# Macaron block on one core: attention's f32 products on quarters of the PE array, and no mask

## The reference, cut to what matters

```python
x = x + 0.5 * ffn(layernorm(x)); x = x + attn(layernorm(x)); x = x + 0.5 * ffn(layernorm(x))
# attn: 16 heads of 32 channels
q, k = relu(to_heads(q)), relu(to_heads(k))
v_pad = jnp.pad(v, ((0, 0), (0, 0), (0, 1), (0, 0)), constant_values=1.0)
vk = jnp.einsum('bhen,bhdn->bhed', v_pad, k)     # per head: 33 x 32, summed over the 512 tokens
out = jnp.einsum('bhed,bhdn->bhen', vk, q)       # per head: 33 values for each token
out = out[:, :, :-1] / (out[:, :, -1:] + 1e-15)
return out.reshape(B, C, N).transpose(0, 2, 1) @ w_proj.T + b_proj
```

## Time and profile before

| | us |
|---|---|
| median of 3 runs (906.39 to 907.36) | 907.1 |
| the profiled execution | 907.83 |
| its span, first to last instruction | 906.0 |
| PE busy | 882.5 (97%) |
| PEld busy | 422.6 (47%) |
| DVE busy | 477.5 (53%) |
| ACT busy | 373.8 (41%) |
| POOL busy | 72.9 (8%) |
| mean granted TensorE clock | 0.994 |

### The profile page before, as it was taken

How to read it: one execution, slowest core, us unless ns; L and a number is a source line. 1 busy time by engine, 2 the same in 40 slices (tenths; PEclk the granted TensorE clock), 3 DMA queues, 4 the chain that set the end, 5 groups by cost and what they waited for, 6 DMA issues and landing times.

```text
span 906.0 us, 11596 instructions
## 1 busy us (share of the span) xinstructions
PE 882.5 (97%) x4288; PEld 422.6 (47%) x4288; DVE 477.5 (53%) x978; ACT 373.8 (41%) x732; POOL 72.9 (8%) x106
## 2 busy tenths in 40 slices
PE   3899999999999999999999999999999999999998
PEld 2544443444444444455555546444444444444443
DVE  7988889844335444525373737454433434433332
ACT  6666666555434445212121212263333344443431
POOL 3110001200000000100000000010000000100000
PEclk9899999999999999999999999999999999999999
DMA  9886614998525678433231404133444433342235
GB/s 279 121 135 129 94 35 90 195 192 179 124 44 119 127 173 157 96 52 47 47 48 20 74 1 83 23 58 59 88 88 88 79 77 71 70 71 59 59 62 135
DMA packets 251383, 84.90 MB, mean 94 GB/s; under 512 B 237888, under 2 KB 240448, under 8 KB 251328
## 3 DMA queue, kind: packets, MB, share of 16 engines
q1 hardware_dynamic: 242704, 70.54, 41.2%
q0 software_dynamic: 3872, 4.72, 3.9%
q10 hardware_dynamic: 4752, 8.91, 3.0%
HBM read 25.43 MB, written 4.19 MB: 33 GB/s over the span
## 4 chain that ended last, share of the span: by engine, by line
PE 94%; DMA 3%; DVE 2%; ACT 1%; issue 0%; ACTq 0%; SPq 0%
PE gate_ps L1063 22%; PE up_ps L1063 22%; PE proj_ps L1077 22%; PE gate_ps L1166 7%; PE up_ps L1166 7%; PE proj_ps L1087 5%; PE proj_ps L1063 4%; PE proj_ps L1177 2%; DMA slots<-slots 1%; DMA xT<-xn 1%; PE sum_ps L1049 1%; PE gate_ps L1102 1%; PE up_ps L1102 1%; DVE slots L796 1%; DMA xs<-in_L_attn_x_dram 1%
## 5 line engine op out<-in xcount | busy, mean ns | idle before, releaser
L1077 PE MATMUL proj_ps<-down_w,slots 128*128 128x512 bf16 x960 | 211.4, 380 | 0.9 <-DMA slots<-slots 0.9
L1063 PE MATMUL gate_ps<-gu_w,xT 128*128 128x512 bf16 (+1 forms) x904 | 203.8, 369 | 2.9 <-DMA xT<-xn 2.9
L1063 PE MATMUL up_ps<-gu_w,xT 128*128 128x512 bf16 (+1 forms) x904 | 203.6, 369 | 0.0
L783 DVE SCALAR_TENSOR_TENSOR slots<-up_ps,silu 128x512 f32<-128x512 f32 x118 | 81.5, 690 | 170.7 <-PE up_ps L1063 153.1
L1077 PEld LDWEIGHTS proj_ps<-down_w,slots 128*128 128x128 f16 x960 | 93.8, 98 | 114.0 <-issue 1.4
L548 ACT ACTIVATE silu<-gate_ps 128x512 f32<-128x512 f32 x118 | 69.7, 590 | 171.4 <-PE gate_ps L1063 171.3
L1063 PEld LDWEIGHTS gate_ps<-gu_w,xT 128*128 128x128 f16 x904 | 86.6, 98 | 102.3 <-DMA xT<-xn 3.0
L1063 PEld LDWEIGHTS up_ps<-gu_w,xT 128*128 128x128 f16 x904 | 86.3, 98 | 99.2
L558 ACT ACTIVATE o_buf<-slots 128x512 f32<-128x512 f32 x128 | 80.4, 628 | 93.7 <-DVE slots L783 92.5
L805 DVE SCALAR_TENSOR_TENSOR xs<-proj_ps,xs 128x512 f32<-128x512 f32 x32 | 22.1, 691 | 134.1 <-PE proj_ps L1077 134.1
L796 DVE SCALAR_TENSOR_TENSOR slots<-slots,inv 128x512 f16<-128x512 f32 x124 | 90.9, 743 | 3.0 <-ACT slots L569 3.0
(11 more groups left out here) (103 smaller groups left out, 746.3 us busy)
## 6 DMA issues: line engine op xcount, KB each, us to landing
out_dram<-xs SPq DMA_DIRECT2D x16, 256.0 KB, 2.4
slots<-in_L_ffn_w_gate_up_dram ACTq DMA_DIRECT2D x6, 512.0 KB, 7.5
aw_raw<-in_L_attn_w_qkv_dram ACTq DMA_DIRECT2D x12, 256.0 KB, 3.0
aw_raw<-in_L_attn_w_qkv_dram SPq DMA_DIRECT2D x12, 256.0 KB, 3.1
xs<-in_L_attn_x_dram SPq DMA_DIRECT2D x2, 1024.0 KB, 6.3
slots<-slots SPq DMA_TRANSPOSE x76, 4.5
xs<-in_L_attn_x_dram ACTq DMA_DIRECT2D x1, 1024.0 KB, 11.8
aw_raw<-in_L_ffn_w_gate_up_dram POOLq DMA_DIRECT2D x4, 256.0 KB, 7.4
```

The lines of the kernel that those rows point to most:

```text
L783: nc.vector.scalar_tensor_tensor(out=h_rows(i, q), in0=bank(up_ps, j), scalar=GU_OUT, in1=silu_rows(j), op0=ALU.mult, op1=ALU.mult).then_i ...
L1063: mm = nc.tensor.matmul(bank(ps, j)[:, first:first + width], xT(m)[:, t, r, k, :], gu_w[:, k, c:c + width], start=(k + r == 0), stop=(k == ...
L1077: mm = nc.tensor.matmul(proj_ps[:, use % 2, :], h_turned(i)[:, r, j, :], down_w[:, j, :], start=(r + j == 0), stop=(r == 1 and j == HC - 1))
```

## The change

K with V uses the array as four column tiles: for each head of a group (`e` = 0 to 3) one matmul of 32 stationary columns and 33 moving ones writes partitions 32e to 32e+31 of `proj_ps`. Q with the result uses four row tiles: for each head the 32 rows of the queries against 33 columns, each row tile into a bank of its own. So 16 f32 matmuls become 64 for K with V in a block, and 4 become 16 for a token tile. The values are stored with a column of ones for every head. The mask, `mask4` and their seven instructions in the prologue (and `mask`'s first ones) go; DVE now only copies the K-V product (two copies for a block).

The order changes with it: K with V comes before the sixth pair of projections (`qkv(b, 5)`), and DVE's copies at the head of step `u` = 5. All of PSUM is now one tensor, and the outputs of a token tile take four banks (one pair's second gate and up bank, and the two of `sum_ps`), the same four for each tile: `attention_output(b, t)` waits until tile `t-1` has been emptied. `gate_done` is signalled at the last group's second head, `up_done` at the end. In block 0 the products of tiles 14 and 15 are split into halves, one half ahead of each token tile.

```diff
-KV_W = P + HPG
-V_W = P + 1
+V_W = HEAD + 1
+G_W = DC * V_W
@@ ScalarE, a token tile
-                    nc.scalar.activation(out_half(t), gate_ps[:, j % 2, 0:2 * KV_W], ACT.Copy).then_inc(gate_used, 1)
+                    nc.scalar.activation(out_half(t), banks[:, 2:4, 0:G_W], ACT.Copy).then_inc(gate_used, 1)
@@ VectorE, u == 5
+                    if u == 5:
+                        for half in range(2):
+                            dve.wait_ge(proj_done, KV_USE[b] + half + 1)
+                            nc.vector.tensor_copy(kv_heads[:, 2 * half:2 * half + 2, :],
+                                                  proj_ps[:, (KV_USE[b] + half) % 2, 0:2 * V_W]
+                                                  .rearrange("p (g m) -> p g m", g=2)).then_inc(proj_used, 1)
@@ TensorE, attention_output
-                j = att_pair(b) + 6 + t
-                for ps, done, used, g0 in ((gate_ps, gate_done, gate_used, 0), (up_ps, up_done, up_used, 2)):
-                    pe.wait_ge(used, j + 1)
-                    for g in (g0, g0 + 1):
-                        c = (g - g0) * KV_W
-                        mm = nc.tensor.matmul(ps[:, j % 2, c:c + KV_W], q_chunk(g)[:, t * P:(t + 1) * P],
-                                              kv_rhs[:, g, :], start=True, stop=True)
-                    mm.then_inc(done, 1)
+                else:
+                    pe.wait_ge(gate_used, att_pair(b) + 6 + t + CREDIT)
+                    pe.wait_ge(up_used, att_pair(b) + 6 + t + CREDIT)
+                for g in range(DC):
+                    for e in range(HPG):
+                        rows = slice(e * HEAD, e * HEAD + HEAD)
+                        mm = nc.tensor.matmul(out_bank(e)[:, g * V_W:g * V_W + V_W], q_chunk(g)[rows, t * P:(t + 1) * P],
+                                              kv_heads[rows, g, :], start=True, stop=True)
+                        if g == DC - 1 and e == 1:
+                            mm.then_inc(gate_done, 1)
+                mm.then_inc(up_done, 1)
@@ TensorE, K with V
-                            mm = nc.tensor.matmul(proj_ps[:, (use + half) % 2, c:c + V_W],
-                                                  k_tile(t)[:, g * P:(g + 1) * P], v_tile(t)[:, g, :],
-                                                  start=(t == 0), stop=(t == TILES - 1))
+                            for e in range(HPG):
+                                mm = nc.tensor.matmul(proj_ps[e * HEAD:e * HEAD + HEAD, (use + half) % 2, c:c + V_W],
+                                                      k_tile(t)[:, g * P + e * HEAD:g * P + e * HEAD + HEAD],
+                                                      v_tile(t)[:, HPG * g + e, :], start=(t == 0),
+                                                      stop=(t == TILES - 1))
@@ TensorE, order
+            for b in range(BLOCKS):
+                for u in range(5):
+                    qkv(b, u)
+                keys_values(b)
+                qkv(b, 5)
+                for t in range(TILES):
+                    if b == 0:
+                        project(14 + t // 2, (t % 2,))
+                    else:
+                        project_attention(b - 1, t)
+                    attention_output(b, t)
```

More of the change, by code:

```diff
@@ L743, in _ @@
             dve.sem_inc(proj_used, CREDIT)
[L744 to L749, removed]
+            step.done(nc.vector.memset(group_ones[:, :], 0.0))
             for h in range(2):
@@ L1005, in _ @@
                         x_low(5 + b, u - 1)
[L1006 to L1026, removed]
-                    for t in range(TILES):
+                if b == 1:
+                    dve.wait_ge(bias_here, 16)
+                for t in range(TILES):
+                    if b:
                         att_out(b - 1, t)
-                        attention_output(b, t)
+                    elif t % 2:
+                        ffn_out(14 + t // 2)
+                    attention_output(b, t)
                 output_low(b, TILES - 1)
@@ L1067, in gate_up, with project @@
                         mm.then_inc(done, 1)
-            def project(i):
+            def project(i, halves=range(2)):
                 use = FFN_USE[i]
@@ L1073, in project @@
                     pe.wait_ge(up_used, 4 * EARLY + CREDIT)
-                for r in range(2):
+                for r in halves:
                     pe.wait_ge(hT_here[r], 16 * (i + 1))
@@ L1078, in project @@
                                               start=(r + j == 0), stop=(r == 1 and j == HC - 1))
-                mm.then_inc(proj_done, 1)
+                if 1 in halves:
+                    mm.then_inc(proj_done, 1)
             def project_attention(b, t):
@@ new lines, in qkv @@
+            def qkv(b, u):
+                for ps, done, used, side in ((gate_ps, gate_done, gate_used, 0), (up_ps, up_done, up_used, 1)):
+                    part, c = u // 2, 2 * (u % 2) + side
+                    pe.wait_ge(used, att_pair(b) + u + 1)
+                    if part == 0:
+                        pe.wait_ge(xT_here[c], 16 * (5 + b))
+                    terms = [(k, r, s) for k in range(DC) for r, s in ((0, 0), (0, 1), (1, 0))]
+                    for m, (k, r, s) in enumerate(terms):
+                        if part < 2:
+                            lhs, dst = xT0[:, c, r, k, :], ps[:, u % 2, :]
+                            rhs = att5[:, s, k, 4 * (part + 1):4 * (part + 2), :].rearrange("p u m -> p (u m)")
+                        else:
+                            lhs, rhs = att5[:, s, k, c, :], xT0[:, :, r, k, :]
+                            dst = ps[:, u % 2, :].rearrange("p (t q) -> p t q", t=TILES)
+                        mm = nc.tensor.matmul(dst, lhs, rhs, start=(m == 0), stop=(m == len(terms) - 1))
+                    mm.then_inc(done, 1)
```

81 lines of the change are left out of this document (29 added, 52 removed).

## The result

| | before | changed |
|---|---|---|
| median, us (4 runs each) | 906.9 | 902.3 (901.08 to 903.61) |
| ratio, 95% interval | | 0.9948 (0.9932 to 0.9963) |
| profiled execution, us | 907.83 | 901.08 |
| its span, us | 906.0 | 899.3 |
| PE busy, us (matmuls recorded) | 882.5 (4288) | 873.0 (4988) |

The change makes the kernel 0.5% faster; I had forecast 912.0 and slower. Six more runs of it, beside eleven of the kernel before, gave 902.45 against 907.36.

The account below looks back on a forecast made before the run. The prediction took PE, full in attention at full clock, as the bound. K with V -1.5 us and outputs +6.4 us made +4.9 us on the median 907.1, forecasting 912.0 us, range 898 to 940.

Parts of the forecast that it names:

- the purse: All of attention's f32 work on PE, the most that could be saved: 28.7 us, 3.2% of the span.
- the sum: Attention's K with V -1.5 us and outputs +6.4 us, together +4.9 us on 907.1, giving 912.0.
- the price of a pair in K with V: Each weight load with its matmul in K with V: 7 to 56 ns possible, 22 ns taken, 2.8 us a block.
- the price of a change of shape: Changing the array's division around each K-V or output stage: 0 or 0.33 to 0.52 us, 0.40 taken, 20 stages.
- outputs, pairs: Output stage of a token tile: still 8 loads of 128 columns per row tile, so 0.90 us as before.
- rival A: Faster: tiles overlap, shape changes cost nothing; K with V 15 ns a pair, 900.4 us, far end 894.8; chance 0.27.
- The 3.2 us that the prediction sets beside its forecast: K with V by the Trainium skill's floor of some 25 ns from start to start, for 128 pairs.
- What moved beside PE: DVE's copies, SP's transposes and the four banks without a second set: nothing lost, 0.5 us of bank slack a tile.
- The order: K with V ahead of the sixth pair, DVE's copies at step u = 5: costed at nothing.
- the forecast: In attention, tiles overlap but shape changes drain the array: 912.0 us, own ends 907 to 919; chance 0.45.
- B: Slower, bound by instruction issue in K with V and outputs: 56 ns a pair, 935.4 us, with drains 944; chance 0.19.
- C: Row tiles' weight loads follow each other: outputs 3.6 us a tile, K with V 3.84, total 951 us; chance 0.09.

Follow-up runs that it names:

- the run with products in between: Changed kernel plus three extra full-array f16 matmuls a token tile, one between each two output groups: 925.40 us; with them all behind the outputs, 913.02.

## Why the prediction was wrong

The bound and the purse were right: PE is full in attention in both kernels, and only its f32 work moved. The change is a gain in one half and a loss in the other, as the sum had it. What failed is the price of a pair in K with V, 22 ns where 9 were measured, and in second place the price of a change of shape, 0.40 us where 0.23 were measured. The sizes:

| term | predicted | measured | times | error, us |
|---|---|---|---|---|
| K with V, pairs | 2.8 (22 ns a pair) | 1.12 (9 ns a pair) | 4 | -6.7 |
| outputs, pairs | 0.90 | 0.90 | 16 | 0 |
| one stage's change of shape | 0.40 | 0.23 | 20 | -3.4 |

(Measured: an output stage costs 3.72 - 2.59 = 1.13 us, eight paces of 0.112 and 0.23. K with V is 1.26 to the next product and 0.09 in front, 1.35, less the same 0.23.) Put into the sum: (1.35 - 3.57) x 4 + (1.13 - 0.90) x 16 = -8.9 + 3.7 = -5.2 us in place of +4.9. The first term by itself turns the sign, since with it right and the edge at 0.40 the sum is -1.8; with the edge alone put right it is +1.5, still slower.

**K with V, the step that failed.** I bounded a pair by 7 and 56 ns and took 22, "between the 15 ns of issue and the 30 of one tile behind the other". But those are two different mechanisms, and a value between them stands for neither. The row for the issue, a second weight load within 15 ns, was an upper bound, and the only evidence on issue that wasn't explained by columns; going by it gives 1.9 us, rival A's price, and with the measured edge (1.9 + 0.23 - 3.57) x 4 + 3.7 = -2.1 us: the sign would have been right; with my own edge of 0.40 it would still have been +1.3. The tiles do work at once, and the engine takes a pair every 9 ns for 128 pairs. The 3.2 us that the prediction sets beside its forecast, 128 starts of 25 ns, are out as well: measured are 1.26.

**The change of shape.** That each change costs something is right and is shown by the run with products in between. It was sized too high: I added the exposed latency of both edges (0.33) and some of the weight loads. Measured is 0.23, 0.09 in front and 0.13 behind, less at each end than the 0.164 of a fully exposed latency. So why it costs just this stays open. That an edge exists agrees with the Trainium skill, "TensorEngine Tiling (Array Packing)", section Key Properties, whose drain on a change of tiling mode shows here as 0.42 us without a weight load.

**The outputs.** Right in the core: same number of 128-column loads one after another, same time, at 33 columns and at 66. The packing gave them nothing, and the edges 0.23 us a tile of loss.

**What moved beside PE.** Nothing, as forecast: no wait of PE for `up_used` or `proj_used` in attention, DVE's copies hidden, the single set of four banks free in time (emptied at 450.29, wanted at 450.92). The order was costed at nothing and is worth next to nothing here; it is worth about 2 us where VectorE has eight copies to do (900.36 against 898.76).

**The rivals.** The result lies between A (900.4) and the forecast: it has pairs still quicker than A's 15 ns and, at a little over half their size, the forecast's edges. The two are independent, and I had tied each pair price to one answer on the edges. The rule of the Trainium skill of one matmul plus a few ns for each further tile ("TensorE: Matmul & The Clock Gate", section Part 3) fits: four matmuls in 0.31 us, each of which lasts up to 0.29. B's 56 ns a pair is out by a factor of six (and its K with V should have read 7.2 us, not 7.1: 128 x 56 ns). C is out by the changed kernel's own outputs, 1.02 us a tile where it had 3.6.

## What to carry to other kernels

In this kernel, cutting the array into tiles helped where both operands of each matmul got shorter: K with V loads 32 columns and streams 33, and fell to 0.38 of its time. Where only the stream got shorter and each tile still loaded 128 columns, nothing was won, and every change of the array's division and back cost about 0.23 us; tiles of 32 x 64, with half the columns in each load, just earned that back. The best here is a mix: K with V in column tiles, and the outputs either on the whole array (898.76 us) or in tiles of 32 x 64 (897.88), both better than the changed kernel's 902.45. So count loaded and streamed columns per tile, set them against 0.23 us a stage and 8 to 10 ns a pair, and order the loops so that neighbouring matmuls fall on different tiles.

## What the runs showed that I had not expected

The granted clock fell where only one row tile worked. In the run with all outputs on row tile 0, PE waited for no other engine, yet (windows, columns as in the earlier trace rows):

```profile
400.00:420.00 20.00, 19.89 (x136) 14.60 (x137) 4.70 (x16) 2.21 (x5) 0.00 (x0) 1.00 0.37 55
420.00:440.00 20.00, 19.78 (x85) 10.63 (x85) 7.71 (x19) 2.85 (x6) 1.35 (x2) 0.74 0.21 39
460.00:500.00 40.00, 40.00 (x204) 24.99 (x202) 14.99 (x34) 4.34 (x9) 0.00 (x0) 0.77 0.21 41
```

The first three stages of block 0, 3.69 us each at 32 rows and 33 columns a pair, still ran at 1.00; during the fourth, 4.74 us long, the granted clock was 0.77, and in the later blocks it fell from the second stage on. In those stretches the clock was at its lower level, 1.2 GHz, for part of the time, and the full-array products behind the stages ran at it too (0.79 from 429 to 440 us, with 18 of them in 6.30 us where 18 at full clock take 3.9). The mean over the span was 0.963 against 0.996 in the changed kernel, so 978.4 x 0.033 = 32 us were lost. With the 43 of the stages that is 75 of the 78 us; attention also began 1 to 4 us later than in the two profiles of the changed kernel. No run here separates what made the clock fall: the few rows, the short streams, or both. In the changed kernel, whose output stages last 1.0 us, the clock stays at 1.00 all through attention. And a pair of a weight load and a matmul was taken every 9 ns for 128 pairs with neighbours on different tiles, where the closest run of pairs in the kernel before was 56 ns apart.
